# The pipeline's steps as counted loops of two, in place of code written out in full

## The reference

```python
x = x + 0.5 * ffn(layernorm(x))      # 6 layers
x = x + attn(layernorm(x))           # linear, a scan over time, linear
x = x + 0.5 * ffn(layernorm(x))      # the same 6 layers and weights again
```

```python
x = attn_layer(shift_tokens(x)) + x  # qkv, 16 heads of 64, window of 32
x = ffn_layer(shift_tokens(x)) + x   # layernorm, W1, a * gelu(gate), W2
```

## Time and profile before

| | |
|---|---|
| Median of 3 runs | 3406.29 us (3406.23 to 3410.3) |
| The profiled execution | 3406.23 us |
| Its span, first to last instruction | 3404.4 us |
| Instructions of PE: matmuls, weight loads | 63324, 63515 |
| Busy share of the span: PE, DVE, ACT, POOL | 97%, 82%, 71%, 65% |
| Mean granted TensorE clock | 0.992 |

### The profile page before, as it was taken

How to read it: one execution, slowest core, us unless ns; L and a number is a source line. 1 busy time by engine, 2 the same in 40 slices (tenths; PEclk the granted TensorE clock), 3 DMA queues, 4 the chain that set the end, 5 groups by cost and what they waited for, 6 DMA issues and landing times. The chain is left out here.

```text
span 3404.4 us, 150755 instructions
## 1 busy us (share of the span) xinstructions
PE 3289.8 (97%) x63324; PEld 2485.3 (73%) x63515; DVE 2794.2 (82%) x6984; ACT 2426.8 (71%) x3769; POOL 2202.1 (65%) x1422
## 2 busy tenths in 40 slices
PE   6999999999999999999999999999999999999998
PEld 4777777777777777777667777777777777777776
DVE  5888888888888888889999888888888888888885
ACT  2777777777777777777667777777777777777775
POOL 4666666666666666666666666666666666666663
PEclk7999999999999999999999999999999999999998
DMA  3111111111111111111111111111111111111111
GB/s 114 51 47 51 48 51 48 50 48 47 51 47 51 48 50 48 51 48 45 46 41 46 51 48 51 48 51 44 48 48 51 48 51 48 51 48 50 50 51 42
DMA packets 199180, 170.06 MB, mean 50 GB/s; under 512 B 139610, under 2 KB 172525, under 8 KB 198509
## 3 DMA queue, kind: packets, MB, share of 16 engines
q1 hardware_dynamic: 193901, 157.05, 16.9%
q10 hardware_dynamic: 4608, 3.34, 0.3%
HBM read 33.38 MB, written 1.05 MB: 10 GB/s over the span
## 5 line engine op out<-in xcount | busy, mean ns | idle before, releaser
L1124 POOL TENSOR_TENSOR rot<-rot,swp 128x1024 f32<-128x1024 f32 x384 | 907.2, 2362 | 142.0 <-DVE rot L901 142.0
L705 ACT ACTIVATE sq<-proj 128x512 f32<-128x512 f32 x768 | 437.8, 596 | 573.5 <-PE proj L503 564.0
L503 PE MATMUL proj<-wq,xsT 128*128 128x512 f32 x1536 | 778.7, 627 | 30.0 <-DVE hT L1037 16.7
L1133 POOL TENSOR_TENSOR rot<-rot,rn 128x1024 f32<-128x1024 f32 x384 | 724.0, 1906 | 0.0
L1114 POOL TENSOR_TENSOR rt<-rt,half 128x1 f32<-128x1 f32 x192 | 105.3, 548 | 848.2 <-DVE rt L983 848.2
L895 DVE TENSOR_TENSOR swp<-proj,tab 128x512 f32<-128x512 f32 x768 | 522.1, 680 | 17.8 <-ACT sq L705 15.7
L901 DVE TENSOR_TENSOR rot<-proj,tab 128x512 f32<-128x512 f32 x768 | 519.0, 676 | 1.8 <-PE tps L514 1.8
L514 PEld LDWEIGHTS tps<-idf,rot 128*128 128x128 f32 x3072 | 361.6, 141 | 207.7 <-issue 203.5
L1037 DVE SCALAR_TENSOR_TENSOR hT<-proj,b1c,fg 114x128 f32<-114x128 f32 (+1 forms) x576 | 166.6, 345 | 413.5 <-ACT fg L769 407.3
L1118 POOL TENSOR_TENSOR prob<-prob,rr 128x1024 f32<-128x1024 f32 x192 | 365.4, 1903 | 187.3 <-DVE rr L995 187.3
L540 PEld LDWEIGHTS sps<-kT,qT 64*32 64x32 f32 x24576 | 365.5, 106 | 131.3 <-issue 130.9
(11 more groups left out here) (113 smaller groups left out, 5687.4 us busy)
## 6 DMA issues: line engine op xcount, KB each, us to landing
vb<-va SPq DMA_DIRECT2D x192, 384.0 KB, 3.5
vb<-va SPq DMA_DIRECT2D x192, 128.0 KB, 3.4
wq<-in_L_ffn_Wqkv SPq DMA_DIRECT2D x95, 192.0 KB
xs<-Z SPq DMA_DIRECT2D x384, 32.0 KB
xs<-Z SPq DMA_DIRECT2D x384, 28.0 KB
xs<-Z SPq DMA_DIRECT2D x384, 3.8 KB
xs<-Z SPq DMA_DIRECT2D x384, 0.2 KB
wo<-in_L_ffn_Wo SPq DMA_DIRECT2D x94, 64.0 KB
```

What stands on the lines that cost most here:

```text
L503: mm(proj[:, c % 2, :], xsT[:, k.parity(L_QKV), :], wq2[:, bass.ds(w + c * 512, 512)], start=True, stop=True).then_inc(p_qkv[c], 1)
L705: fn(sq[:, c * 512:(c + 1) * 512], proj[:, c % 2, :], ACT.Square).then_inc(a_sq[c], 1)
L1124: g_.tensor_tensor(r, r, swp[:, g * INNER:(g + 1) * INNER], ALU.add).then_inc(g_add[g], 1)
L1133: g_.tensor_tensor(r, r, rn[:, g * HEADS:(g + 1) * HEADS].unsqueeze(2) .to_broadcast([P, HEADS, DH]), ALU.mult).then_inc(g_nm[g], 1)
```

## The change

PE now goes through `pipeline_by_layer`, and the other four engines through a `pipeline` that loops.

```diff
         def pipeline(eng, step, between=None, mid_end=MID_END, end=T, last=T + L_F2):
 
             unrolled(eng, step, 0, FRONT, between)
-            unrolled(eng, step, FRONT, last)
+            looped(eng, step, FRONT, MID)
+            unrolled(eng, step, MID, mid_end)
+            looped(eng, step, mid_end, end)
+            unrolled(eng, step, end, last)
@@
             pe.wait_ge(c_zero, 1)
             pe.wait_ge(c_zero2, 1)
-            pipeline(pe, step, between)
+            pipeline_by_layer(pe, step, between)
```

## The result

The changed kernel takes 3538.03 us (median of 4 runs, 3534.35 to 3539.02) where the one before, run beside it, takes 3406.26: a ratio of 1.038, 95% interval 1.037 to 1.040, slower by 132 us. The forecast was slower by 494 us. The direction was right. The price was nearly four times too high, and most of what was paid went to something else than forecast.

A forecast was written before the change was run, and what follows sets the result against it. PE was taken to bound the kernel, so idle time added to PE lengthens the whole. Branch fetches and operations 317, next block 50, body 24, clock 58 and other engines 45 sum to 494: 3406 + 494 = 3900 us, range 3500 to 4160.

The forecast's parts named there:

- part 1: At PE's 69 branches back: the target block is no longer held and must be fetched, 4.3 us each.
- rival B: PE's loop body stays in its instruction memory, so refetches and code stalls in looped steps go: 3415 us, chance 0.09.
- Part 3: On PE behind each branch target: the next block arrives late, in the transposes or late in attention, 50 us.
- part 5: PE's clock after waits at the branch: half speed costs 1.7 us, at half of the 69 branches, 58 us.
- Part 2: PE's six sequencer operations at each branch back, 0.11 us each: 0.3 to 0.4 us after the sequencer's lead.
- Part 4: Extra register operations inside PE's loop body, at the step boundary and ahead of projections: 0.3 us x 80, 24 us.
- Part 6: Other engines' turns: DVE's fetch and operations delay the rotation PE's fourth projection awaits, 0.6 us at 75 branches, 45 us.
- Part 7: Savings on PE: waits left out were already counted; code stalls in scores and attention stay as they are on average.
- D: PE's body stays in memory and all register operations hide behind its work: faster, 3370 us, chance 0.06.
- C: At PE's branch back, the target's fetch waits for one under way: 207 us more, 4107 us, chance 0.10.
- the forecast's own range: Range of the main case, the target fetched at every PE branch back: 3680 to 4150 us, chance 0.72.
- a branch that costs part of a fetch: Partial case at PE's branch back: only part of a fetch is paid, 3560 us or so, chance 0.03.

## Why the prediction was wrong

The step that failed is part 1: that PE holds just the block it is in and the next one, so that the target of every branch back must be fetched. The price was right, the condition wrong. With bodies of 10.9 blocks a branch back takes 4.75 us in the median against my 4.3; with this kernel's 5.5 blocks it takes 0.22. I read "only the next block is fetched ahead" off the stalls, which no run speaks against, and took it for "only two blocks are kept", which does not follow. My one argument against rival B, that a memory of eight blocks would make it easy to be more than one ahead, was a guess about a design and not a row. The Trainium skill had both readings, "Runtime: NRT & Kernel Launch", section "Instruction fetch mechanics": its rule that a taken branch out of the current two pages forces a fetch is contradicted by the 146 packets and the 0.22 us. Its memory of 2048 instructions for PE agrees with both runs, 1,404 that stay and 2,800 that don't.

Point by point:
- Part 1, 297 us: nothing. Part 3, 50 us, and part 5, 58 us: nothing, since no block is fetched and no pause exceeds 1.0 us at the turn. Parts 1 and 5 both appear in the run with four steps in the body; part 3 was not seen apart.
- Part 2, 0.3 to 0.4 at each turn: 0.5 measured. Its 0.11 for one operation is about right for the simple ones, but the branch takes 0.22 and the six need 1.0 us.
- Part 4, 24 us: not seen by itself. Parts 2 and 4 with the code stalls given back make rival B's sum, 45 - 36 = +9 us; PE's loops alone cost 12.
- Part 6, 45 us: the right engine by the wrong cause and too small. DVE's 70 us come in every step; half of them are shown to be address arithmetic between a wait and the operation that others wait for, the half in the even steps is put down to the same by likeness. I had asked only what happens at its turn. The 0.4 us that I gave DVE's rotation to spare were not there in full either: the rotation ends at 1303.35, and the fourth projection's first load begins at 1303.40, held up by it. PE's new wait for a rotation, my sign for this part, did appear, but 39 of its 43 places belong to ACT's table load. That load, 33 to 39 us, is what my statement that ACT turns "idle for most of it" missed.
- Part 7: wrong, "the stalls stay as they are on average". They went, as rival B said.

B's mechanism for PE is what happened, and its 3415 is PE's loops alone (3412). D, that the register operations hide, fails by the 80 pauses of 0.5 us. C's wait of 7 us did not show even where a fetch is needed: the longest pause of PE at a turn of the run with four steps is 5.8. B left out DVE and ACT altogether: I had let part 6 go with part 1, as if the other engines could only lose by fetches.

The parts measured one by one are PE 12, DVE 70, ACT's table load 33 by the ratios or 39 by the steps, ACT otherwise -3, POOL and SP -6 (0.19% of 3400): 106 to 112 of 131 (3.84%). Without PE they give 94 to 100, and the run of the other four took 103, so most of what is missing needs PE in loops as well. Undoing DVE in the whole is worth 81 and not 70, so some 11 of the missing 19 to 25 us seem to arise where DVE's delay meets PE's, though that figure is as large as its noise. A reading that fits: alone, DVE's lateness partly falls into PE's stalls for code, which are not there any more when PE loops too. That was argued and not tested, and the rest is left open.

That the time lies in the range, 3500 to 4160, is luck. The lower end was far under the forecast's own range (from 3680) to take in a branch that costs part of a fetch, and no such cost exists here; what filled the gap were DVE and ACT, for reasons that the forecast did not have. The case of B alone, at 3415, lay outside the range. The sign that I had named for being wrong altogether, under 1 us of idle time of PE at the branch, did come.

## What to carry to other kernels

Whether a loop's branch is cheap depends on whether the body stays in the sequencer's memory: count the instruction packets before and after, and don't infer what is kept from how far ahead it fetches. Then price the loop on every engine and at every step, not at the turn: each address that depends on the loop's register is sequencer work, and it costs nothing only where it does not stand between a wait and the operation that someone else waits for; computing it ahead of a wait that is there anyway brings it back. And look at what the compiler places at the head of a loop that is entered from a different state than its own end leaves, such as a function table; starting the loop an iteration later was the whole repair here.

## What the runs showed of the hardware

- A branch back on PE takes 0.22 us with a body of 1,404 instructions (median; 146 packets in all) and 3.4 to 5.5 with one of 2,800 (579 packets). On DVE, with a body of 154 instructions, more than its block of 128, no block is fetched twice either: q14 falls from 162 packets to 101 when DVE alone loops, and by the counts of the two traces its program is some 7,700 instructions shorter, 60 blocks.
- Code written out is not free on PE: by the rows of before it is fetched one block ahead, and PE stalls in dense stretches, 38.7 us in the scores alone; loops that stay in memory bring that down to 6.3.
- A packed register operation takes 0.06 us on DVE in the one case and 0.30 in the other of the two ahead of a rotation; the program has a simple sum and an address with remainders and quotients there; a function table load on ACT takes 1.28 us wherever it stands.
